# Batchwise residual, norms, projection and rotation inside the attentions, and an unrolled self-attention

## The reference

```python
x = x + xattn(layernorm(x), ctx)      # 16 heads of 64; a null key and value; out projection, then a layernorm of its own
z = layernorm(x)
h = rmsnorm(z, ln1_w)
q, k = rope(h @ wq, h @ wk); v = h @ wv          # 16 query heads, 8 key heads, 8 wide
ao = softmax(causal(q k^T / sqrt(8))) v          # two query heads share a key head
z = z + ao @ wo
h = rmsnorm(z, ln2_w)                            # then top 2 of 8 experts, gate, up, down
return x + z + moe(h)
```

## Time and profile before

| | us |
|---|---|
| median of 3 runs (lowest, highest) | 682.86 (681.18, 684.12) |
| the profiled execution | 680.71 |
| its span, and mean granted clock share | 678.9, 0.945 |
| busy PE, DVE, ACT, POOL | 580.8, 512.8, 423.3, 310.9 |

### The profile page before, as it was taken

The page is one execution under the profiler, slowest core; times in us unless marked ns, Lnnn a source line. Parts: engine busy times, 40 slices in busy tenths (PEclk is TensorE's granted clock), DMA queues, the critical chain, the costliest instruction groups (busy, mean ns, idle before and its releaser), DMA issues. The chain is left out here.

```text
span 678.9 us, 11861 instructions
## 1 busy us (share of the span) xinstructions
PE 580.8 (86%) x3500; PEld 457.3 (67%) x3500; DVE 512.8 (76%) x1127; ACT 423.3 (62%) x1030; POOL 310.9 (46%) x555
## 2 busy tenths in 40 slices
PE   2969999998999989999873458999984898788996
PEld 2747777776787768778662355666664786666885
DVE  4657777868678677777955577999954699869995
ACT  3547777767777667877850257888844555444653
POOL 1346667756667656766753547213302504223000
PEclk9979999999999999999986778999987899888999
DMA  7020000001000000000000020000000220200001
GB/s 253 1 56 1 3 30 1 1 2 32 1 1 2 1 0 3 0 1 1 2 1 1 0 90 1 1 1 0 0 1 13 76 74 1 83 0 0 0 0 31
DMA packets 14386, 13.05 MB, mean 19 GB/s; under 512 B 2048, under 2 KB 13696, under 8 KB 14336
## 3 DMA queue, kind: packets, MB, share of 16 engines
q1 hardware_dynamic: 14032, 12.41, 5.7%
q10 hardware_dynamic: 304, 0.03, 0.0%
HBM read 11.92 MB, written 0.52 MB: 18 GB/s over the span
## 5 line engine op out<-in xcount | busy, mean ns | idle before, releaser
L809 POOL TENSOR_SCALAR attn_probs<-attn_probs,rinv 128x512 f32<-128x512 f32 x128 | 87.5, 697 | 23.0 <-DVE rinv L724 22.8
L733 DVE TENSOR_TENSOR pT_lo<-bank,pT_hi 128x512 fp32r<-128x512 f32 x128 | 87.5, 685 | 7.5 <-ACT pT_hi L627 5.5
L709 DVE TENSOR_REDUCE neg_max<-bank 128x1 f32<-128x512 f32 x128 | 82.1, 683 | 11.2 <-PE bank L478 11.2
L611 ACT ACTIVATE attn_probs<-bank,bias 128x512 f32<-128x512 f32 x128 | 87.4, 687 | 4.9 <-DVE bias L717 4.6
L627 ACT ACTIVATE pT_hi<-bank 128x512 fp32r<-128x512 f32 x128 | 73.2, 595 | 14.2 <-PE bank L493 14.0
L493 PE MATMUL bank<-ident,attn_probs 128*128 128x128 f32 x512 | 76.3, 281 | 5.6 <-POOL attn_probs L809 5.3
L493 PEld LDWEIGHTS bank<-ident,attn_probs 128*128 128x128 f32 x512 | 56.6, 142 | 29.0 <-issue 17.8
L1658 ACT ACTIVATE act_hi<-act_f 128x512 fp32r<-128x512 f32 x56 | 35.4, 632 | 57.2 <-DVE act_f L1701 56.9
L512 PE MATMUL bank<-pT_hi,vals 128*128 128x256 f32 x256 | 65.6, 288 | 5.5 <-DVE p0T_lo L750 3.4
L512 PE MATMUL bank<-pT_lo,vals 128*128 128x256 f32 x256 | 64.2, 283 | 0.0
L512 PEld LDWEIGHTS bank<-pT_hi,vals 128*128 128x128 f32 x256 | 48.8, 191 | 8.1 <-issue 4.5
(11 more groups left out here) (273 smaller groups left out, 1658.4 us busy)
## 6 DMA issues: line engine op xcount, KB each, us to landing
ctx_raw<-in_ctx SPq DMA_DIRECT2D x4, 512.0 KB, 4.8
wkv_raw<-in_L_xattn_Wkv SPq DMA_DIRECT2D x2, 1024.0 KB, 10.1
gu_raw<-in_L_ffn_w_gate SPq DMA_DIRECT2D x4, 448.0 KB, 3.6
gu_raw<-in_L_ffn_w_up SPq DMA_DIRECT2D x4, 448.0 KB, 4.3
dn_raw<-in_L_ffn_w_down SPq DMA_DIRECT2D x4, 448.0 KB, 5.2
x<-in_x SPq DMA_DIRECT2D x1, 512.0 KB, 6.4
wq_raw<-in_L_xattn_Wq SPq DMA_DIRECT2D x1, 512.0 KB, 9.8
wout_raw<-in_L_xattn_Wout SPq DMA_DIRECT2D x1, 512.0 KB, 12.1
```

The source lines that it names most:

```text
L611: act.activation(probs[:, g % 2, i, t, :], score_bank(G, i)[:, :], ACT.Exp, bias=bias[:, t, h:h + 1], scale=X_SCALE, accum_out=row_sum[:, ...
L709: dve.tensor_reduce(neg_max[:, t, h:h + 1], score_bank(G, i)[:, :], AX_X, ALU.max, negate=True).then_inc(max_s, 1)
L733: dve.tensor_tensor(pT_lo[:, i, 2 * half:2 * half + 2, :], t_bank[half][:, :].rearrange("p (j n) -> p j n", j=2), f(pT_hi[:, i, 2 * half:2 ...
L809: pool.tensor_scalar(probs[:, g % 2, i, t, :], probs[:, g % 2, i, t, :], rinv[:, t, h:h + 1], 1.0, ALU.mult, ALU.mult).then_inc(p_norm_s, 1)
```

## The change

`residual_and_projections` is gone. Its work is done batch by batch: for batches 0 to 2 at fixed steps of the cross-attention, counted from the batch's last pair, for batch 3 in the self-attention. The projection is split in hi and lo: three matmuls per tile (`project_qkv`), the weights' split made by POOL at the start. The null probabilities' copy and split move from ACT and DVE on the bank to ACT on the bank and POOL on the copy, one step earlier, and the context's step changes places. `x1` shares `x`, and `yT` holds two batches.

```diff
+def project_qkv(pe, k, b, out):
+
+    pe.wait_ge(k.hT_lo_s, b + 1)
+    for t in range(QT):
+        cols = slice(t * P, (t + 1) * P)
+        for m, (x, w) in enumerate(((k.hT_hi, k.wqkv_hi), (k.hT_lo, k.wqkv_hi), (k.hT_hi, k.wqkv_lo))):
+            last = pe.matmul(out[:, t * N:(t + 1) * N], x[:, cols], w[:, :], start=m == 0, stop=m == 2)
+    last.then_inc(k.qkv_ps, 1)
...
+def add_residual(dve, k, b):
+
+    for t in tiles_of(b):
+        last = dve.scalar_tensor_tensor(k.y_tok[:, t % QT, :], k.y_tok[:, t % QT, :], k.mv_y[:, t, 0:1], k.scale_row[:, :],
+                                        ALU.subtract, ALU.mult)
+    linked_dve(dve, k, last)
+    dve.wait_ge(k.y_rstd, b + 1)
+    dve.wait_ge(k.x_bias_s, 1)
+    for t in tiles_of(b):
+        last = dve.scalar_tensor_tensor(k.x1[:, t, :], k.y_tok[:, t % QT, :], k.rstd_y[:, t:t + 1], k.x1[:, t, :],
+                                        ALU.mult, ALU.add)
+    last.then_inc(k.x1_s, 1)
...
+def rotate(engine, k, b, heads, dst, link, done):
...
+    for a, c in ((0, HD // 2), (HD // 2, 0)):
+        last = engine.tensor_tensor(out[:, :, :, a:a + HD // 2], src[:, :, :, c:c + HD // 2],
+                                    sin[:, :, :, a:a + HD // 2].broadcast_to([P, QT, n, HD // 2]), ALU.mult)
+    link(engine, k, last)
+    link(engine, k, engine.tensor_tensor(src, src, cos.broadcast_to([P, QT, n, HD]), ALU.mult))
+    engine.tensor_tensor(dst, src, out, ALU.add).then_inc(done, 1)
...
+def split_hT(pool, k, b):
+
+    pool.wait_ge(k.hT_s, b + 1)
+    if b:
+        pool.wait_ge(k.qkv_ps, b)
+    linked(pool, k, pool.tensor_scalar(k.hT_hi[:, :], k.hT[:, :], 1.0, 1.0, ALU.mult, ALU.mult))
+    pool.tensor_tensor(k.hT_lo[:, :], k.hT[:, :], f(k.hT_hi[:, :]), ALU.subtract).then_inc(k.hT_lo_s, 1)
...
+        def finishing(s, step):
+
+            b, r = divmod(s - step, HP)
+            return b - 1 if r == 0 and 1 <= b < B else None
+
+        Y_TURN, Y_MOMENTS, Y_SCALE, ADD, X1_MOMENTS, X1_SCALE, H_SCALE, MAKE_H, H_TURN, H_SPLIT, QKV, ROTATE = (
+            3, 4, 5, 5, 6, 6, 7, 7, 8, 9, 9, 10)
```

The steps of PE, then of DVE, then of POOL in the cross-attention:

```diff
                 if after_context(s):
                     keys_unit(s)
+                if values_late(s):
                     weighted_values(s - 1, 1)
                     values_unit(s)
                 else:
                     values_unit(s)
                     weighted_values(s - 1, 1)
+                finish_batch(s)
+                null_probs(s)
                 transpose_probs(s, 1, 0)
                 project_q(s + 2)
-                null_probs(s)
+                weighted_values(s, 0)
                 context_unit(s, 0)
-                weighted_values(s, 0)
                 scores(s + 2, 0)
```

```diff
+                finish_early(s)
                 o_halves(s - 1, 0)
                 o_halves(s - 1, 1)
                 q_tail(s + 2)
-                null_tail(s)
+                inverse_sum(s + 1, 0)
+                finish_batch(s)
+                probs_tail(s, 1, 0)
                 context_tail(s, 0)
-                inverse_sum(s + 1, 0)
-                probs_tail(s, 1, 0)
```

```diff
                 null_weight(s, 1)
+                null_split(s)
+                finish_batch(s)
                 whole_sum(s + 1, 0)
```

On PE:

```diff
+        STEPS = range(-3, SA + 3)
+        FEATURE_STEPS = (0, 1, 3, 4)
+        LATE_BATCH = B - 1
+        POST_STEPS = {-3: "y", 5: "h", 7: "qkv"}
...
+            def tokens_first(h):
+
+                out = free_bank("tokens", h)
+                pe.wait_ge(zero_s, 1)
+                pe.wait_ge(o_s, HELD * (h + 1))
                 for t in range(QT):
                     for j in range(REP):
...
+                        last = pe.transpose(out[:, (t * REP + j) * P:(t * REP + j + 1) * P],
+                                            oT[:, h % 2, j * N + t * P:j * N + (t + 1) * P], k.ident[:, :])
+                last.then_inc(tok_ps, 1)
...
+            for s in STEPS:
+                transpose_keys0(s)
+                extra(s)
+                if s == -3:
+                    for u in range(4):
+                        features(0, u, s_bank[u])
+                transpose_keys1(s)
+                weighted_values(s - 1)
+                scores(s + 3)
```

On DVE, where `extra` stands between the two lo parts of a pair:

```diff
+            def extra(s):
+                if s == 0:
+                    add_residual(dve, k, LATE_BATCH)
+                    x1_moments(dve, k, LATE_BATCH)
+                if s == 3:
+                    make_h(dve, k, LATE_BATCH)
+                if s == 9:
+                    rotate_queries(dve, k, LATE_BATCH)
+                if features_at(s) is not None and features_at(s)[1] >= 2:
+                    keys_first(*features_at(s), a_of("features", features_at(s)))
+                if tokens_at(s) is not None:
+                    attention_sums(tokens_at(s))
```

POOL's list in the self-attention:

```diff
+            key_quads(0)
+            scale_y(pool, k, LATE_BATCH)
+            query_quads(1)
+            key_quads(1)
+            pool.memset(oT[:, :, :], 0.0).then_inc(zero_s, 1)
+            pool.memset(f(v_all[:, :, :, 2 * HD]), 1.0)
+            values(0, LATE_BATCH)
+            scale_x1(pool, k, LATE_BATCH)
+            scale_h(pool, k, LATE_BATCH)
+            query_quads(2)
+            key_quads(2)
+            split_hT(pool, k, LATE_BATCH)
+            attention_out(0)
+            rotate_keys(pool, k, LATE_BATCH)
+            values(LATE_BATCH, B)
+            query_quads(3)
+            key_quads(3)
+            attention_out(1)
             split_pair(pool, k, 0, 0)
```

More of the change, by code:

```diff
@@ L314, in _, with over_tiles, tiles_of, tokens @@
                 unit(n)
+def over_tiles(row, tiles=TT):
+    return row[:, :].unsqueeze(1).broadcast_to([P, tiles, D])
+def tiles_of(b):
+    return range(b * QT, (b + 1) * QT)
+def tokens(k, b):
+    return k.early[:, b, :] if b < B - 1 else k.late[:, 0, :]
+def rotated_queries(k, b):
+    return tokens(k, b)[:, 0:QT * FH * HD].rearrange("p (t h d) -> p t h d", t=QT, h=FH)
+def rotated_keys(k, b):
+    return tokens(k, b)[:, QT * FH * HD:QT * (FH + KV) * HD].rearrange("p (t h d) -> p t h d", t=QT, h=KV)
@@ new lines, in raw_values, with turn_y, turn_h @@
+def raw_values(k, b):
+    return tokens(k, b)[:, QT * (FH + KV) * HD:].rearrange("p (t h d) -> p t h d", t=QT, h=KV)
+def turn_y(pe, k, b, out):
+    pe.wait_ge(k.y_whole, b + 1)
+    for t in range(QT):
+        last = pe.transpose(out[:, t * P:(t + 1) * P], k.yT[:, b % 2, t * P:(t + 1) * P], k.ident[:, :])
+    last.then_inc(k.y_tok_ps, 1)
+def turn_h(pe, k, b, out):
+    pe.wait_ge(k.h_s, b + 1)
+    for t in range(QT):
+        last = pe.transpose(out[:, t * P:(t + 1) * P], k.h_rms[:, t, :], k.ident[:, :])
+    last.then_inc(k.hT_ps, 1)
@@ L1216, in queries_first @@
[L1216 to L1226 removed]
+            def queries_first(b, u, src):
+                act.wait_ge(f_ps, 4 * b + u + 1)
+                act.activation(qT[:, 2 * u:2 * u + 2, b * N:(b + 1) * N], src[:, :].rearrange("p (g n) -> p g n", g=2), ACT.Copy)\
+                    .then_inc(qT_s, 1)
@@ L1246, in steps @@
-            def steps(b, which, last_batch=False):
-                end = KV if last_batch else which.stop + 2
-                for p in which:
-                    if 0 <= p < end:
-                        probs_head(b, p)
-                    if 0 <= p + 2 < end:
-                        exponentials(b, p + 2)
-                    if 0 <= p - 1 < end and p % 2:
-                        output_copy(b, p - 1)
-            quad_heads(0)
-            act.activation(v_all[:, :, :, 0:HD], k.qkv[:, :, FH + KV:, :], ACT.Copy)
@@ new lines, in _ @@
+            for a in (0, 2):
+                last = act.activation(query_slot(0, a), query_heads(0), ACT.Copy, scale=F_SCALE)
+            last.then_inc(q_hi_s, 1)
+            for s in STEPS:
+                probs_head(s)
+                extra(s)
+                if s == -3:
+                    for u in range(2):
+                        queries_first(0, u, s_bank[u])
+                    act.wait_ge(mask_in, 16)
+                    act.activation(mask[:, :], mask_f[:, :], ACT.Copy).then_inc(consts_s, 1)
+                    act.activation(ident_b[:, :], k.ident[:, :], ACT.Copy).then_inc(consts_s, 1)
+                exponentials(s + 2)
+                output_copy(s - 1)
@@ new lines, in _ @@
+            dve.wait_ge(q_hi_s, 1)
+            for a in (1, 3):
+                last = dve.scalar_tensor_tensor(query_slot(0, a), query_heads(0), F_SCALE, f(query_slot(0, 0)), ALU.mult, ALU.subtract)
+            last.then_inc(q_quad_s, 1)
+            for s in STEPS:
+                if s == -3:
+                    y_moments(dve, k, LATE_BATCH)
+                    for u in range(2, 4):
+                        keys_first(0, u, s_bank[u])
+                maxima(s + 2)
+                probs_tail(s)
+                extra(s)
+                probs_tail_1(s)
+                output_copy(s - 1)
```

786 lines of the change are left out of this document (412 added, 374 removed).

## The result

The changed kernel takes **670.24 us** (median of 4 runs, 670.07 to 674.27) beside 682.02 for the kernel before (680.52 to 684.12, 4 runs): ratio 0.984, 95% interval 0.9802 to 0.9879. The forecast was 655.5 with 670 as its high end. The direction was right, the gain less than half of what was forecast.

What follows compares the result with a forecast made beforehand. PE bounds mid cross-attention and pair loop, DVE the last four cross-attention steps, a three-engine chain the gap. 0.7 + 3.5 + 2.5 + 6.0 - 38.5 - 1.7 + 0.2 = -27.3; with 2.15 for the median, 655.5 us, range 642 to 670.

Steps and rivals of the forecast that it cites:

- Parts 4 and 5: Drain after the cross-attention, +6.0 us; gap before the first self-attention scores, -38.5 us, with 7.4 left of 45.9.
- Part 2: Batches 0 and 1 and batch 2's first step inside full cross-attention steps: +3.5 us.
- The gains on the null and context waits: Cross-attention: PE's null wait goes, 3.4 us, and 2.0 of the 3.1 before the context's transposes.
- its sign of being wrong at the root: Steps with a station longer by the whole station, or first scores over 12 us after yT's last addition.
- Part 3: Batch 2 in the light cross-attention steps, DVE's moments, residual and h counted in full: +2.5 us.
- Contention: DVE's two-input operations in residuals and rotations held by POOL's memory use; the sum had 0.11 us each, 3.5 in all.
- The rival's 670.5: Contention at its worst: 32 DVE operations cost 13.3 us more, the pair loop's 1.7 gain goes; chance 0.12.
- Part 6: Self-attention pair loop: -1.7 us, 31 starts in 82.0 after 83.7; PE's sum 78.0, DVE's 79.2.
- the rival of the lumps: Pair loop: extras in 21 of 32 steps don't overlap, loop takes 93 us, total 666.5; chance 0.14.

Runs made afterwards that it cites:

- e14: Changed kernel with one edit: POOL splits h before the null probabilities, no waits added; 663.7 us.
- e4: Changed kernel with POOL's values split waiting for DVE in the cross-attention steps of residual and rotation; 668.3 us.
- e5: Changed kernel with the projection of batches 0 and 1 one pair later, the rotation one later again; 668.1 us.
- e1: The changed kernel run once more, nothing edited; 670.76 us.
- e12: Changed kernel with the orders and waits of e6, e14 and e8 together; 657.74 us, ratio 0.9661 to the kernel before.
- e13: Changed kernel with the orders of e14 and e8, and DVE's residual and rotation at the end of its step; 663.3 us.
- e15: As e12, but the rotation alone at the end of DVE's step, without POOL's wait there; 657.60 us, ratio 0.9627 to the kernel before.
- e6: As e4, but POOL normalises the next pair before its wait and the values split; 667.2 us.
- e7: Changed kernel, pair loop: ACT and DVE copy the output first, DVE takes its half bank first, PE's extras follow the weighted values; 670.7 us.
- e8: Changed kernel, pair loop: PE's scores before the weighted values, DVE's maxima three pairs ahead and before its output copy; 666.9 us.
- e10: As e8, with every extra at the end of its pair-loop step on all three engines; 675.6 us.
- e11: Changed kernel with DVE's residual of batches 0 to 2 on one column of 128 and one addition for their query rotation; 663.8 us.

## Why the prediction was right or wrong

**Parts 4 and 5 held.** The gap: 45.9 to 6.9, forecast 7.4. The drain: 5.9 more, forecast 6.0, made of the pieces named. PE's 3.52 us for hT_lo are POOL's split of the last output and the two splits behind it, 1.2 each, and 0.84 for ACT follows before the output projection. The key quads' broadcast did not double them; on POOL they were off the path.

**Part 2 failed at "it hides ... cost nothing" for POOL.** It priced POOL's pieces against the idle time of an average step (1.71). But in one step the null split and the split of h come together, and PE asks for the second just then. "Up to 0.3 where two splits meet" measured 1.3 us for the wait at pairs 19 and 27, and 1.3 more for the clock behind it at one of the two (e14, e4). The rows for it were there: the order of POOL's list and 1.2 us a split. The clock after a wait of PE was in no term of the sum. The gains on the null and context waits came near their forecast of 5.4: as far as their places tell, 3.1 at pairs 5, 11 and 21 (-0.86, -1.52, -0.7) and 1.5 at pairs 19 and 27, which e5 lays bare.

**Part 2 failed again at DVE's slack of "about 1.0 in a step".** The charge was 1.5 a batch. Measured are 1.86 + 2.32 a batch for residual and rotation (e1), and 1.45 + 1.74 in e12, where the four operations of a group take about 1.7 and 1.8 us from the first start to the last end. So nearly all of the time for which they occupy DVE is lost. Between the reciprocal and the next pair's maxima the step leaves DVE next to nothing, and at the end of the step nothing either, where the next step pays (e13, e15). The idle 0.53 before the keys' lo was read as slack, and these pieces could not use it; why not is argued from the order, not shown. This is what the prediction had set as its sign of being wrong at the root: steps longer by the whole station. Part 3 charged DVE's work in full and stands: 1.56 for the residual's 1.2. DVE at 75% busy is no engine with a quarter of its time to give.

**Contention was right in kind, and the sum had it too small.** The sum took 0.11 an operation, 3.5 in all. In e1 the 30 moved operations of batches 0 to 2 take 8.8 us more than they do undisturbed: 5.9 in residual and rotation, where one operation is held for up to 1.0 us, and 2.9 in h, which was said to fit. Not all of it reaches the path. Taking the 5.9 away brought 1.1 us in the five steps of e4, where POOL is late instead, and taking 4.0 away brought 1.9 in those of e6. The hold on h stands in every trace (1.36 to 1.40 us instead of 0.33), and so do the 0.54 to 0.58 us at pairs 17 and 25; no run takes it away, so its price, and with it the split between DVE's plain work and the holding, is open. The rival's 670.5 equals the measured time by accident. It stood for 13.3 us of contention on the path, and the pair loop, which it left as it was before, lost 5.9 by another cause.

**Part 6 failed at the plain step.** The step of 2.21 for PE was right as a sum: plain steps of 2.1 to 2.2 exist (e7, e8, e10). What failed is "I take 82.0" from the largest sum: with PE, DVE and ACT at 2.2 to 2.4 us each, the steps took 2.4 to 3.3 (one 1.6) even in the last quarter, where few steps have an extra and the rival of the lumps has little to say. The time went into waits that the orders of three engines pass to each other, hidden before under PE's work in steps of 2.73. Reordering alone gave back 3.4 of the 7.6 missing. The other 4.2 were not recovered: DVE's wait for the hi copy and PE's for DVE's output copy remain in e8, and five of the first six steps stay at 3.0 to 3.8. These have the late batch's work, and the first two the lower clock (0.50 up to 400.7 in e8; pair 2 starts at 402.5). Which of these holds the most is open.

**The sum, mended:** -27.3 + 10.2 (cross-attention) + 7.6 (pair loop) - 0.4 (drain, gap, pair 0 and tail) is -9.9; from the profiled execution's 680.71 that gives 670.8, and e1 took 670.76. The 2.15 that the forecast added for the median has no counterpart after: the median there is 0.5 below e1.

## What to carry to other kernels

Work that is moved into a loop "because an engine idles there" must be laid against the order of that engine's list in the very step where it lands, and against who waits next; the busy share of a long stretch says only that the time exists, not that it can be used. Where the engines' sums come within 10% of each other, the largest sum is a bound and not a forecast: look for two engines whose last instruction in a step stands before the other's first, and take such inputs a step further ahead. When a wait of TensorE is priced, look whether the granted clock falls behind it; and when an order is improved, whether it does so in every step, since a few long waits with the clock behind them can eat more than the whole gain (e10). And hold single executions against each other by parts, not by their totals: here the stretch behind the pair loop, with the same work in every run, varied by 6 us.

## What the hardware did that was not expected

- A DVE operation with two inputs on a single column was held for the whole 1.28 us of a POOL instruction (e11): 1.38 us for two, where two full ones take 0.60 when POOL is kept away (e4's 340 ns each, less the overlap).
- After a wait of 1.9 us, around which PE worked 0.45 of 2 us, the clock stood at half for about 3 us and cost 1.3 us more, in eight traces of ten. Elsewhere it fell in some executions and not in others: e1 ahead of pair 21 and e14 ahead of pair 29 lost 1.5 us more than e4 and e12 do there, with the clock at 0.50 for 3.4 us in each.
